# Two of four gathered, weighted rows summed by TensorE in PSUM instead of by GpSimd and VectorE, in a four-layer transformer on one core

## The reference

```
sim = einsum('btphn,hkpn->pbthk', q, keys)          # 128 keys per half and head
... top 8 of each half, then top 8 of the 64 sums -> indices, scores
de, ue = down_embed[indices], up_embed[indices]      # 32 rows of 256 each, per token
ew = einsum('btd,bthkd->bthk', hidden_states, de)
ew = silu(ew) * softmax(scores)
experts_states = einsum('bthk,bthkd->btd', ew, ue)   # sum over 32 weighted rows
```

## Time and profile before

| | us |
|---|---|
| median of 3 runs | 1735.56 |
| range of the runs | 1729.33 to 1751.61 |
| profiled execution, its own time | 1747.5 |
| span in that profile | 1745.5 |
| busy PE / DVE / ACT / POOL | 1320.8 / 1127.6 / 810.4 / 693.0 |
| mean granted clock of TensorE, share of full | 0.859 |

### The profile page before, as it was taken

How to read it: one execution, slowest core, us unless ns; L and a number is a source line. 1 busy time by engine, 2 the same in 40 slices (tenths; PEclk the granted TensorE clock), 3 DMA queues, 4 the chain that set the end, 5 groups by cost and what they waited for, 6 DMA issues and landing times.

```text
span 1745.5 us, 18805 instructions
## 1 busy us (share of the span) xinstructions
PE 1320.8 (76%) x5858; PEld 661.1 (38%) x5858; DVE 1127.6 (65%) x2929; ACT 810.4 (46%) x2052; POOL 693.0 (40%) x705
## 2 busy tenths in 40 slices
PE   5889886747778586447667568677879978887998
PEld 3245443333344343213323333433444434533444
DVE  5542317579996777897898897996542433426365
ACT  2345442646658576438556649558234330210010
POOL 2000000468878777648868688884000010000000
PEclk8699898968899698668878789898889989997999
DMA  6000000455557556736546766663000121021000
GB/s 229 6 1 1 10 7 1 113 143 158 162 164 162 156 163 193 152 97 173 174 127 183 194 181 172 180 170 101 7 16 1 67 49 32 1 49 40 4 13 24
DMA packets 59380, 169.07 MB, mean 97 GB/s; under 512 B 15632, under 2 KB 20304, under 8 KB 58640
## 3 DMA queue, kind: packets, MB, share of 16 engines
q0 software_dynamic: 40960, 134.25, 28.9%
q1 hardware_dynamic: 18320, 33.61, 6.1%
HBM read 163.00 MB, written 4.82 MB: 96 GB/s over the span
## 4 chain that ended last, share of the span: by engine, by line
PE 40%; DVE 27%; ACT 13%; issue 9%; DMA 5%; POOL 3%; another core or an unknown queue 2%; SPq 1%; DVEq 0%; ACTq 0%; POOLq 0%
PE psum L1159 5%; PE psum L1025 4%; ACT bufR L1184 4%; DVE bufR L1389 3%; DVE bufB L1516 3%; POOL bufR L1826 3%; ACT bufR L1256 3%; PE psum L960 2%; PE psum L1103 2%; PE psum L952 2%; PE psum L1037 2%; DVE x_sb L1407 2%; PE psum L1082 2%; PE psum L829 2%
## 5 line engine op out<-in xcount | busy, mean ns | idle before, releaser
L1826 POOL DMA_INDIRECT bufR<-in_table,rowid x512 | 554.0, 1082 | 238.7 <-issue 127.5
L1184 ACT ACTIVATE bufR<-bufR 128x256 f32<-128x256 f32 x512 | 205.6, 405 | 85.1 <-DVE bufR L1389 69.7
L1389 DVE TENSOR_TENSOR bufR<-bufR 128x1024 f32<-128x1024 f32 x128 | 160.7, 1258 | 26.4 <-DMA bufR<-in_table,rowid 23.7
L829 PE MATMUL psum<-bufB 32*128 32x308 f32 x768 | 99.5, 596 | 101.4 <-DVE bufB L1516 76.3
L1025 PE MATMUL psum<-xtf,wf 128*128 128x512 f32 x320 | 153.5, 624 | 23.6 <-DVE x_sb L1452 11.5
L1516 DVE TENSOR_REDUCE bufB<-psum 128x8 f32<-128x1232 f32 x96 | 137.9, 1436 | 44.4 <-PE psum L829 42.9
L1853 POOL TENSOR_TENSOR x_sb<-x_sb,wattn 128x256 f32<-128x256 f32 x16 | 11.0, 723 | 310.0 <-DMA wattn<-in_attn 186.2
L1452 DVE TENSOR_TENSOR x_sb<-x_sb,psum 128x256 f32<-128x256 f32 x128 | 50.6, 417 | 118.3 <-PE psum L960 67.8
L1846 POOL TENSOR_TENSOR x_sb<-x_sb,wattn 128x256 f32<-128x256 f32 x32 | 23.5, 765 | 236.4 <-DMA wattn<-in_attn 158.3
L1786 DVE SCALAR_TENSOR_TENSOR x_sb<-psum,bufR,x_sb 128x256 f32<-128x256 f32 x128 | 61.9, 484 | 77.3 <-PE psum L1159 70.8
L1256 ACT ACTIVATE bufR<-psum 128x1024 f32<-128x1024 f32 x96 | 92.8, 1019 | 39.3 <-PE psum L855 37.3
(11 more groups left out here) (236 smaller groups left out, 2582.0 us busy)
## 6 DMA issues: line engine op xcount, KB each, us to landing
bufR<-in_table,rowid POOLq DMA_INDIRECT x512
wf<-in_ffn SPq DMA_DIRECT2D x2, 2304.0 KB, 18.7
bufR<-in_ffn SPq DMA_DIRECT2D x1, 2696.5 KB, 16.9
wattn<-in_attn SPq DMA_DIRECT2D x4, 641.0 KB
wf<-in_rope SPq DMA_DIRECT2D x4, 512.0 KB
bufB<-in_ffn SPq DMA_DIRECT2D x1, 2048.0 KB, 8.5
scr_corr<-bufR SPq DMA_DIRECT2D x16, 128.0 KB, 2.4
bufR<-scr_corr SPq DMA_DIRECT2D x4, 512.0 KB
```

The lines of the kernel that those rows point to most:

```text
L829: ins = mm(psum[:, z, 0:PAR * S], q[r, g, i * P:(i + 1) * P], keysm[r, g, b, :, 0:S], start=True, stop=True)
L1184: own.mark(act(row, row, ACT.Identity, accum_out=dots[:, g % 4, j:j + 1]))
L1389: tt(rows, rows, cast(xg[c % 2][:, i, :].unsqueeze(1), [P, GRP, D]), ALU.mult).then_inc(f1_mu, 1)
L1826: eng.indirect_dma_start(ring[:, s * GRP + j, :], None, io["table"], bass.IndirectOffsetOnAxis(ap=rowid[c % 2][:, at + j:at + j + 1], axis ...
```

## The change

- Rows 2 and 3 of each unit (`PE_ROWS`) are now summed by PE. ACT writes the identity matrix times the row's weights (one weight per partition) into the first 128 columns of that row's down half, which is used up by then. The result is a diagonal matrix of the weights. PE multiplies it with the up half (128 x 128 by 128 x 256, fp32) and accumulates all 8 units of a tile in bank 5. The signal `f1_pe` frees these two rows.
- DVE adds two rows instead of three. `add_half` adds bank 5 to x.
- POOL has no adds in the fetch any more; `half_sum` is gone.
- Bank 5 therefore belongs to the fetch. Transposes (of `a` and `f` fronts), queries, and the values of the context all go through bank 4, one half at a time: the second half waits until the first has been copied out. The fronts of layer 3 (`q`, `z`) still use both banks, and the last users of banks 4 and 5 wait for the end of the fetch (`ring_left`).
- Items and durations of the planner follow, so it makes a new order.

```diff
+PE_ROWS = (2, 3)
...
-    PE=dict(kv=3.9, X=1.45, Q=4.1, ...
+    PE=dict(kv=2.0, ax=1.0, X=0.75, Q=2.05, ...
...
-             th=2.05, sc=0.5, ...
+             th=2.75, sc=0.6, ...
-             ew=0.41, ad=1.6, ga=0.42, Q=5.6, ...
+             ew=0.41, ad=1.08, ga=0.42, Q=2.8, ...
...
-            p = add("POOL", ("ad", g), 0.8, s, g and ("POOL", ("ad", g - 1)), first and g and ("DVE", ("ga", g - 1)))
+            p = add("PE", ("ax", g), 1.0, s, first and g and ("DVE", ("ga", g - 1)))
...
+            def transposes(tgt, layer, c, kt):
+                f, at = front_of[tgt, layer, c], bank_x(tgt, kt)
+                if kt == 0:
+                    eng.wait_ge(ld_const, 16)
+                    shared_banks(("X", tgt, layer, c))
+                elif at == bank_x(tgt, 0):
+                    eng.wait_ge(fr_ev, KT * f + kt)
                 eng.wait_ge(fr_xn, TI * (f + 1))
+                for i in range(TI):
+                    ins = eng.transpose(psum[:, at, i * P:(i + 1) * P], normed(tgt, layer, c)[:, i, kt * P:(kt + 1) * P], ident)
+                ins.then_inc(fr_tp, 1)
...
+            def project(layer, c, g):
+                k = chunk(layer, c)
+                if g == 0:
+                    shared_banks(("Q", layer, c))
...
+                else:
+                    eng.wait_ge(sk_p, 2 * k + 1)
                 for kt in range(KT):
+                    ins = mm(bank(4), w("wq")[:, kt, g * P:(g + 1) * P], xta[:, kt, :], start=kt == 0, stop=kt == KT - 1)
                 ins.then_inc(sk_q, 1)
...
+            def add_rows(g):
+                at, s_ = GRP * (g % SLOTS), g % NG
+                eng.wait_ge(f1_wt, g + 1)
+                if s_ == 0 and g:
+                    eng.wait_ge(f1_tile, g // NG)
+                for j in PE_ROWS:
+                    ins = mm(psum[:, 5, 0:D], ring[:, at + j, 0:P], ring[:, at + j, D:2 * D], start=s_ == 0 and j == PE_ROWS[0],
+                             stop=s_ == NG - 1 and j == PE_ROWS[-1])
+                ins.then_inc(f1_pe, 1)
...
-                for j in (3,):
-                    row = ring[:, at + j, D:2 * D]
-                    ins = act(row, row, ACT.Copy, scale=ew[:, g % 4, j:j + 1])
+                for j in PE_ROWS:
+                    ins = act(ring[:, at + j, 0:P], ident, ACT.Copy, scale=ew[:, g % 4, j:j + 1])
...
                 own.link(stt(x, ring[:, at, D:2 * D], ew[:, g % 4, 0:1], x, ALU.mult, ALU.add))
-                own.link(stt(x, ring[:, at + 1, D:2 * D], ew[:, g % 4, 1:2], x, ALU.mult, ALU.add))
-                stt(x, ring[:, at + 2, D:2 * D], ew[:, g % 4, 2:3], x, ALU.mult, ALU.add).then_inc(f1_acc, 1)
+                stt(x, ring[:, at + 1, D:2 * D], ew[:, g % 4, 1:2], x, ALU.mult, ALU.add).then_inc(f1_acc, 1)
...
-                tt(x, x, half_sum[:, :], ALU.add).then_inc(f1_tile, 1)
+                tt(x, x, psum[:, 5, 0:D], ALU.add).then_inc(f1_tile, 1)
...
-                    if g >= SLOTS and j == GRP - 1:
-                        eng.wait_ge(f1_half, g - SLOTS + 1)
+                    if g >= SLOTS and j == PE_ROWS[0]:
+                        eng.wait_ge(f1_pe, g - SLOTS + 1)
```

More of the change, by code:

```diff
@@ L147, in front @@
         xt = "xta" if tgt in ("a", "q") or (tgt, c % 2) == ("z", 1) else "xtf"
-        x1 = add("PE", ("X",) + item, 1.3, n4, banks[0], ("SP", ("in", "const")), use[xt])
+        late = tgt in ("q", "z")
+        for kt in range(KT):
+            x1 = add("PE", ("X",) + item + (kt,), 0.7, n4, banks[0], ("SP", ("in", "const")), use[xt], kt and not late and x2)
+            x2 = add("ACT", ("X",) + item + (kt,), 0.6, x1)
         use["x1"] = x1
@@ L151, in front @@
             use["xa"] = x1
-        x2 = add("ACT", ("X",) + item, 1.25, x1)
         banks[0] = x2
@@ L158, in queries @@
         shared.append(("Q",) + item)
-        q1 = add("PE", ("Q",) + item, 3.6, xt, ld["q", PIECE_AT[k]])
-        use["xta"] = q1
-        old = k >= 2 and ("PE", ("r",) + A_ORDER[k - 2] + (1,))
-        if layer < 2:
-            banks[0] = add("ACT", ("Q",) + item, 1.3, q1, old)
-        else:
-            banks[0] = add("DVE", ("Q",) + item, 5.0, q1, old, ld["rope", c])
+        old = k >= 2 and ("PE", ("r",) + A_ORDER[k - 2] + (1,))
+        for g in range(2):
+            q1 = add("PE", ("Q",) + item + (g,), 1.8, xt, ld["q", PIECE_AT[k]], banks[0])
+            if layer < 2:
+                banks[0] = add("ACT", ("Q",) + item + (g,), 0.7, q1, old)
+            else:
+                banks[0] = add("DVE", ("Q",) + item + (g,), 2.8, q1, old, ld["rope", c])
+        use["xta"] = q1
         return banks[0]
@@ L248, in ffn1 @@
             i = g // NG % TI
-            f = add("POOL", ("gf", g), 4.0, t, back >= 0 and ("POOL", ("ad", back)), back >= 0 and ("DVE", ("ad", back)),
+            f = add("POOL", ("gf", g), 4.0, t, back >= 0 and ("PE", ("ax", back)), back >= 0 and ("DVE", ("ad", back)),
                     land=LAND)
@@ new lines, in kv @@
+            def kv(layer, b, part):
+                j = B * layer + b
+                if part == 0:
+                    eng.wait_ge(ld_const, 16)
+                    eng.wait_ge(ld_ctx, 32)
+                    eng.wait_ge(ld_kv, 16 * (layer + 1))
+                    shared_banks(("kv", layer, b))
+                    for g in range(2):
+                        for kt in range(KT):
+                            ins = mm(psum[:, 4, g * S:(g + 1) * S], w("wk")[:, kt, g * P:(g + 1) * P], ctxt[:, kt, b * S:(b + 1) * S],
+                                     start=kt == 0, stop=kt == KT - 1)
+                    ins.then_inc(kv_k, 1)
+                    return
+                eng.wait_ge(kv_kt, 2 * (j + 1))
@@ L1854, in add_bias3 @@
                 ins.then_inc(o3_bo, 1)
-            work = {"gf": fetch, "ad": add_rows, "bo": add_bias, "bo3": add_bias3}
+            work = {"gf": fetch, "bo": add_bias, "bo3": add_bias3}
             for item in order["POOL"]:
```

133 lines of the change are left out of this document (48 added, 85 removed).

## The result

The changed kernel took **1806.2 us** (median, 1799.0 to 1817.6), the kernel before beside it 1732.4 (1727.1 to 1751.6): a ratio of **1.041, 95% interval 1.031 to 1.051**. The forecast was 1662 and faster; the time lies above the range and on the other side. The profiled execution took 1810.8 us (span 1809.0).

What follows compares the result with a forecast made beforehand. POOL bounds the fetch stage before, PE after the change. From 1747.5 us, the stage falls from 875 to 805, the tail loses 11, one bank adds 8, the median takes off 12: 1662 us, range 1605 to 1745.

Steps and rivals of the forecast that it cites:

- How full can its stream be?: In the fetch stage PE was taken as 86.5% busy, like the last stretch, giving 770 to 845 us.
- POOL sets the pace: In the fetch stage before, POOL's work, issue gaps and waits fill 860 of 875 us, 6.84 us per unit.
- PE becomes the bound, stage 805: In the changed fetch stage PE needs 666 to 731 us; stage 805, above POOL's 717, so 70 us are gained.
- rival B: Fetch stage limited by five ring slots: rounds of 33 us, stage 845, time 1702, within 2%; chance 0.2.
- The tail, -11: Planner moves PE's matmul groups and transposes ahead of the fetch's end, so the stretch after it loses 11 us.
- Sums: On PE in the fetch stage, 128 sums at 1.0 us each, 128 us; upper bound 230.
- Diagonals: On ACT, one weighted row becomes two writes of 128 columns, 0.353 us each, 26 us more in all.
- One bank: Transposes, queries and values in series through one bank cost 8 us outside the fetch stage, at most 17.
- The longer DVE adds: DVE adds lengthened beside POOL's adds in the fetch stage go too, another 10 to 20 us, 15 taken.
- C: PE waits at its new sums for ACT's diagonals: stage 982, time 1840; chance 0.15 for over 2% slower.
- activity releases the throttle: PE's clock in the fetch stage, 0.82 before, rises as PE gets denser, so added sums partly pay for themselves.

Runs made afterwards that it cites:

- e5: The kernel before in its own order, adds of rows 2 and 3 cut to 4 of 256 columns on DVE and POOL: 1663.2 us, ratio 0.972.
- e15: The kernel before in its own order, adds of rows 2 and 3 cut to 4 columns on DVE and POOL, run again on chip D: 1668.8 us, 0.972.
- e8: The kernel before without the sums of rows 2 and 3 anywhere, ordered anew with 5.6 us for four fetches instead of 5.1: 1676.3 us, ratio 0.980.
- e2: The kernel before with only the one bank for transposes, queries and values, fetch unchanged, ordered anew: 1753.6 us, ratio 1.016.
- e14: The changed kernel ordered anew with the planner's duration for four fetches at 5.6 us instead of 5.1, run on chip D: 1691.2 us, ratio 0.986.
- e12: The changed kernel ordered anew with the planner's duration for four fetches at 5.35 us instead of 5.1: 1830.6 us, ratio 1.056.

## Why the prediction was wrong

**The step that failed** is the answer to "How full can its stream be?": a density of 86.5%, taken from the stretch behind the fetches, put on the stretch of the fetches. The donor stretch has no fetch in it, and stands come only beside fetches. With them PE reached 74.6%, idle 233.7 us against my 107: its signals came up to 12 us late, and DVE, ACT and then PE itself waited for them. But the density fails without them too: on chip D the same code had PE idle for 157.6 us, 80.9% busy. The 277 us of stands are a union over three engines, and part of them would have been idle anyway; what they cost is the difference between the two runs of the same code, 97 us of the stage and 106 of the span (1809.0 against 1702.9). They cost the kernel before little: it ran at 1710.6 to 1714.3 on chips B and D and at 1725.2 to 1735.6 elsewhere, some 20 us for 145 us of stands. That it loses less is measured; that its PE, idle for 284 us, had room to absorb them is my reading.

**POOL sets the pace.** Right for the kernel before, as far as the runs go. With some 60 us of POOL's adds cut and everything else kept (e5, e15; DVE's third add goes too) 47 and 45 us came back, and POOL was still full. What I left out is the supply of indices: POOL at its floor gets to the third chunk before DVE has them, 65.3 us too early in e8, 34.0 in the changed kernel and 32.7 on chip D. No wait of this kind stood in the rows of before.

**PE becomes the bound, stage 805.** On a chip without stands the stage took 823.3: PE's need of 665.8 is the low end of my 666 to 731, its clock 0.90 where I had hoped for 0.92, its density 80.9%. POOL lost 69.8 us to the sums and 26.1 to DVE there, over the 80 that I had set as rival B's mark, and 32.7 to the indices; with 549.9 busy and 144.1 of "issue" that is the whole stage. 1703 is within the range of 1605 to 1745 and 1 us from rival B's 1702. That is in part luck: B had a stage of 845 by rounds of 33 us, and it was 823 with rounds of 30.0. And the forecast was still 41 us low there (1703 against 1662), with the kernel before 21 us faster than the 1735.6 I started from: in place of 4% faster, the same within 1%.

**The tail, -11.** Wrong in sign: 558.9 and 551.1 for 548.5. The planner's order does put those groups ahead of the last sums, but PE is no longer that far in its order when the last fetch ends: 2996 matmuls in the stage, where 2553 and the 512 sums make 3065. In the changed kernel the last sum ran at 1291.1, 41 us behind the last fetch. A place in an order is not a place in time.

**The terms.** Sums 1.16 us each (1.0 taken, 1.0 to 1.8): right. Diagonals 0.34 us busy each (0.353): right. One bank: +8, measured 7 to 10 ahead of the fetches alone and 28 in all in e2; too low, as I counted ten fronts outside the stage and nothing inside it. The longer DVE adds went, and more than I took: DVE's stage fell by 107 us, 38 beyond the removed line, for the 15 of my sum. In the kernel before, the 54 adds of the three lines that lasted over 1.2 times their median all ran beside an add or a copy of POOL. L1430's mean is still 532 ns for two of its 128:

```profile
L1430 DVE SCALAR_TENSOR_TENSOR x_sb<-bufR,ew,x_sb x128: 483/485/3462, 359.1 to 1263.2; 128x256 f32<-128x256 f32 x128
```

The two took 3.38 and 3.46 us, each beside four of POOL's bias adds.

**The rivals.** C named the right size of idle (above 177 us slower than before; 233.7) but the wrong mechanism: PE stood 12.0 us for the diagonals, and the mark of over 60 before the new line was not reached (35.1). B's mark was reached, 165 us of waits for slots; a round from first fetch to the end of PE's sum took 35.2 us on the mean, and 35.2 / 5 x 128 = 900 of the 920 us. But on chip D the round is 30.0 with the same ring. The ring passes the late signals on to the fetches; it does not make them.

The Trainium skill ("TensorE: Matmul & The Clock Gate", "Part 1: The HAM clock gate") was cited with its rule that activity releases the throttle. The trace agrees in direction, 0.86 and 0.90 for 0.82 with PE's busy share up from 68% to 75% and 81%; it was worth little against the stands.

## What to carry to other kernels

Before putting a density of one stretch on another, look at what the donor stretch lacks, and add up the waits without a releaser by stretch: dozens of small waits were 145 us here. When two sets of runs disagree, put the same kernel on both chips before explaining anything by the edit; here one number in a table seemed to be worth 5% and was worth 0.7%. Before counting on what an engine gives up, work out what it will wait for at its new pace: POOL without its adds stood 65 us for indices that had never been late before (e8). And a cut that leaves an instruction in place leaves part of its time: POOL's adds of 4 columns took 0.33 us, those of 256 columns 0.83.

## What the runs showed of the hardware

Chips differ in a way that no count of instructions shows. The kernel before differs by 1.4% between them, the changed kernel by 6% (1702.9 and 1806.2). What goes with it is that PE's semaphore updates come late, by up to 12 us after the modelled ends of the matmuls, only while GpSimd's gathers run, with POOL going on, and that some updates are missing from the trace in the same stage (387 of 466 recorded in the changed kernel, 466 of 466 on chip D). Two chips of four have it, and so have both traces of the result. Each chip ran within a few minutes, so the chip and the hour of its runs cannot be told apart. What makes the signals late is open: something else at work on the chip is not excluded, nor is a part of the recording itself, as every execution on record was run with its span and clock recorded. The few recorded packets of the instruction queues don't fall on the stands more often than chance would have it (13 of 60 in the changed kernel's stage, with stands and the microsecond ahead of them 37% of its time), and full DMA engines alone don't do it (chip D).

A DVE instruction can be held by a tensor operation of GpSimd: an add of 128 x 256 that takes 0.485 us took 3.46 beside four bias adds.

The best kernel measured that computes everything is e14, the changed kernel with `gf=5.6`, 0.986 of before on a chip without stands. No kernel beat the one before on a chip with them, where e12, its neighbour with 5.35, ran at 1.056.
